# New orders of an audio tower's five engines, with PE's fillers ahead of the gate logits and the spread weights in four transfers

## What is computed

```python
patches = x[:, idx, :].reshape(B, 92, 512)
h = einsum('bpf,df->bpd', patches, W) + b
# attention, 8 heads of 64, on layernorm(h)
dots = einsum('bhid,bhjd->bhij', q, k) * scale
attn = softmax(dots)
attn = einsum('bhij,hg->bgij', attn, reattn_w)          # mixes the heads
attn = layernorm over the heads of attn * ln_g + ln_b
h = h + (attn @ v) @ w_out.T + b_out
# experts, on x = layernorm(h): two of eight for each token
scores = softmax(x @ gate_w.T);  topk_w, topk_i = top_k(scores, 2)
combine = topk_w / (sum(topk_w) + 1e-20), at topk_i
y = sum over e of combine[e] * (relu(x @ w1[e] + b1[e]) @ w2[e] + b2[e])
h = h + y + relu(x @ sw1 + sb1) @ sw2 + sb2
```

## Time and profile before

| what | value |
|---|---|
| median of 3 executions | 692.98 us (692.62 to 693.32) |
| the profiled execution, its own time | 693.01 us |
| its span | 691.2 us |
| PE busy | 646.2 us, 93% |
| DVE busy | 504.5 us, 73% |
| ACT busy | 446.1 us, 65% |
| POOL busy | 419.8 us, 61% |
| chain that ended last, by engine | PE 69%, DVE 21%, issue 3%, ACT 3%, POOL 2% |
| costliest group off PE | POOL act_split_lo, 127.5 us |
| spread, each | 1472 KB, 6.2 us from issue to landing |

### The profile page before, as it was taken

One profiled execution on the slowest core, in us unless ns is written; L12 is line 12 of the kernel. 1 busy time (PEld: TensorE's weight loads), 2 busy tenths in 40 slices (PEclk: granted clock), 3 DMA queues, 4 the chain that ended last, 5 costly groups with the idle time before them and its releaser, 6 DMA issues.

```text
span 691.2 us, 16491 instructions
## 1 busy us (share of the span) xinstructions
PE 646.2 (93%) x5918; PEld 591.8 (86%) x5918; DVE 504.5 (73%) x1432; ACT 446.1 (65%) x1430; POOL 419.8 (61%) x568
## 2 busy tenths in 40 slices
...
DMA packets 16753, 37.39 MB, mean 54 GB/s; under 512 B 1504, under 2 KB 13728, under 8 KB 14624
## 3 DMA queue, kind: packets, MB, share of 16 engines
...
...
## 4 chain that ended last, share of the span: by engine, by line
PE 69%; DVE 21%; issue 3%; ACT 3%; POOL 2%; DMA 1%; ACTq 0%; POOLq 0%; DVEq 0%
PE ps_mix L634 13%; PE ps_fill L414 12%; PE ps_fill L416 10%; PE ps_fill L415 10%; PE ps_dots L623 9%; PE ps_av L642 7%; PE ps_fill L563 5%; DVE key L1021 4%; DVE shift_l L1010 2%; DVE aT L1065 2%; DVE x2T_lo L1122 1%; PE ps_fill L734 1%; ACT x2T_hi L859 1%; DMA spread<-weights 1%; DVE hot L1016 1%
## 5 line engine op out<-in xcount | busy, mean ns | idle before, releaser
L486 POOL TENSOR_TENSOR act_split_lo<-act,act_split_hi 128x736 fp32r<-128x736 f32 (+1 forms) x80 | 127.5, 1603 | 15.0 <-ACT act_split_hi L842 15.0
L776 ACT ACTIVATE ex<-ps_dots,negmax 128x92 f32<-128x92 f32 x384 | 124.3, 342 | 6.9 <-DVE negmax L1046 6.5
L1194 POOL TENSOR_TENSOR sum<-sq 92x384 f32<-92x384 f32 x64 | 64.6, 1009 | 93.3 <-ACT sq L784 93.3
L634 PE MATMUL ps_mix<-mixk,probs 128*92 128x128 f32 x768 | 99.0, 280 | 11.4 <-DVE aT L1067 11.4
L1188 POOL TENSOR_TENSOR probs<-ex,rinv 128x552 f32<-128x552 f32 x64 | 71.0, 1109 | 51.9 <-DVE rinv L1052 51.9
L634 PEld LDWEIGHTS ps_mix<-mixk,probs 128*92 128x92 f32 x768 | 87.3, 162 | 17.3 <-issue 12.7
L1141 DVE SCALAR_TENSOR_TENSOR act<-ps_fill,b_neg,spread 128x368 f32<-128x368 f32 x128 | 70.5, 591 | 24.6 <-PE ps_fill L416 17.6
L776 ACT ACTIVATION_READ_ACCUMULATOR ex<-ps_dots,negmax 128x1 f32 x384 | 81.2, 212 | 0.0
L623 PE MATMUL ps_dots<-xT,yT 128*64 128x92 f32 x1536 | 74.5, 247 | 2.0 <-ACT ex L776 2.0
L623 PEld LDWEIGHTS ps_dots<-xT,yT 128*64 128x64 f32 x1536 | 64.9, 138 | 5.4 <-ACT ex L776 3.1
L1065 DVE TENSOR_TENSOR aT<-ps_mix,arstd 92x360 f32<-92x360 f32 x128 | 61.7, 522 | 6.8 <-ACT arstd L794 4.5
...
## 6 DMA issues: line engine op xcount, KB each, us to landing
spread<-weights SPq DMA_DIRECT2D x16, 1472.0 KB, 6.2
...
spread<-tok_raw SPq DMA_DIRECT2D x1, 256.0 KB, 3.5
```

The source lines that it names most:

```text
L486: eng.tensor_tensor(lo, act1[:, two, :], hi.bitcast(F32), ALU.subtract).then_inc(units_ready, 1)
L634: last = pe.matmul(ps_mix[0:N, c // HALF, o:o + 128], probs[:, (s - 1) % 2, c, :], mixk[:, :, :].rearrange("p g i -> p (g i)"), start=True ...
L776: last = act.activation(ex[:, s % 2, c, :], ps_dots[:, c // HALF, o:o + N], ACT.Exp, bias=negmax[:, c:c + 1], accum_out=sums[:, s % 2, c:c ...
L1194: pool.tensor_tensor(sum4[:, :, :, :], sq[:, :, 0:4, :], sq[:, :, 4:8, :], ALU.add)\
```

## The change

1. New orders in `SETUP`, `ORDER_0`, `STEPS` and `ORDERS_END`, and new counts in `KEEP_BUSY`.
2. The eight fillers stand ahead of `RT` instead of ahead of `CT`, in RT's bank (`FILL_BUSY`).
3. The logits are made by one reduce over the two rows of products instead of a copy and an add.
4. spread comes in four transfers of 368 KB, two experts each, each with a semaphore; the acts of an expert wait for its own.
5. In G = 17, the low halves of `H1` and `H3` are made on DVE instead of POOL (`VECTOR_UNITS`).

```diff
 STEPS = [
-    ("dots", 0), ("max", 0), ("av", 0), ("ev", 0), ("mix", 0), ("exa", 0), "Z5", "Z3", "Z2", ("sq", 0), ("exb", 0),
...
+    ("dots", 0), ("max", 0), ("exa", 0), "Z6", ("mix", 0), ("sq", 0), "Z5", "Z3", ("exb", 0), "Z2", "XE", ("inv", 0),
...
+VECTOR_UNITS = ("H1", "H3")
...
-ROUTE_BUSY = 8
...
+FILL_BUSY = {"RT": 8}
...
-                    sp.dma_start(spread[:, :, :].rearrange("p e w -> p (e w)"),
-                                 bass.AP(tensor=weights_dram.tensor, offset=0, ap=[[0, 128], [1, E * W]]))\
-                      .then_inc(weights_spread, 16)
+                    for k in range(E // 2):
+                        two = bass.AP(tensor=weights_dram.tensor, offset=2 * W * k, ap=[[0, 128], [W, 2], [1, W]])
+                        sp.dma_start(spread[:, 2 * k:2 * k + 2, :], two).then_inc(weights_spread[k], 16)
...
+                if FILL_BUSY.get(step, 0) and 0 <= g and G < LAST - 2:
+                    wait_free(pe, step, G)
+                    columns = w1_split[0][:, 0:4, :].rearrange("p e w -> p (e w)")
+                    for _ in range(FILL_BUSY[step]):
+                        pe.matmul(bank(step)[:, 0:W], columns[:, 0:128], columns[:, 0:W], start=True, stop=True)
+                if step == "CT":
+                    pe.wait_ge(route, N_ROUTE * (g + 1))
...
-                    columns = w1_split[0][:, 0:4, :].rearrange("p e w -> p (e w)")
-                    for _ in range(ROUTE_BUSY if g >= 0 and G < LAST - 2 else 0):
-                        pe.matmul(ps[:, 0:W], columns[:, 0:128], columns[:, 0:W], start=True, stop=True)
-                    pe.wait_ge(route, N_ROUTE * (g + 1))
...
-                    for ahead, unit in enumerate(units):
-                        pe.wait_ge(units_ready, len(UNITS) * g + ahead + 1)
+                    on_pool = [unit for unit in units if not on_vector(unit, G)]
+                    aside = [unit for unit in units if on_vector(unit, G)]
+                    for unit in units:
+                        if on_vector(unit, G):
+                            pe.wait_ge(vector_units, aside.index(unit) + 1)
+                        else:
+                            pe.wait_ge(units_ready, len(UNITS) * g + on_pool.index(unit) + 1)
...
-                    sums = bank("RT")[:, 0:2 * TILES * E].rearrange("p (t r e) -> p r t e", t=TILES, r=2)
-                    dve.tensor_copy(logit[:, :, :], sums[:, 1, :, :]).then_inc(logit_low, 1)
-                    dve.wait_ge(logit_low, g + 1)
-                    dve.tensor_tensor(logit[:, :, :], sums[:, 0, :, :], logit[:, :, :], ALU.add)\
-                       .then_inc(emptied[BANK["RT"]], 1)
+                    sums = bank("RT")[:, 0:2 * TILES * E].rearrange("p (t r e) -> p t e r", t=TILES, r=2)
+                    dve.tensor_reduce(logit[:, :, :], sums, AX_X, ALU.add).then_inc(emptied[BANK["RT"]], 1)
...
+                if on_vector(step, G):
+                    low_units(dve, step, G).then_inc(vector_units, 1)
...
-                    if step == [other for other in order(G) if other in EXPERTS][0]:
-                        dve.wait_ge(weights_spread, 16 * g + 16)
+                    experts = [other for other in order(G) if other in EXPERTS]
+                    if step == experts[0]:
                         at_least(dve, units_ready, len(UNITS) * g)
+                    if step == [other for other in experts if int(other[1]) // 2 == e // 2][0]:
+                        dve.wait_ge(weights_spread[e // 2], 16 * g + 16)
```

More of the change, by code:

```diff
@@ L32 @@
 N_ROUTE = 18
+ROUTED = {"RT": 2, "R2": 12, "R3": N_ROUTE}
 COPY = 32
@@ L75 @@
 STEPS = [
[8 rows of a table removed]
[3 rows of a table added]
+    "OP", ("rstd", 1), "shift", ("exa", 2), ("exb", 2), "TK", ("scale", 1), "TH2", "TH", "Z4", ("dots", 3),
[4 rows of a table added]
 ]
@@ L128 @@
 ORDER_0 = [
-    ("dots", 0), ("max", 0), ("exa", 0), ("exb", 0), ("inv", 0), "XE", "XO", "shift", "V3", ("dots", 1), ("max", 1),
-    ("mix", 1), ("exa", 1), ("sq", 1), ("exb", 1), "TK", ("rstd", 1), ("inv", 1), ("dots", 2), ("max", 2),
[3 rows of a table removed]
-    ("inv", 3), ("scale", 3), "BS",
+    "XE", "XO", "shift", ("dots", 0), ("max", 0), ("exa", 0), ("exb", 0), "TK", ("inv", 0), "V2", ("dots", 1),
+    ("mix", 1), ("max", 1), ("exa", 1), ("sq", 1), ("exb", 1), ("inv", 1), "TH", ("dots", 2), ("max", 2),
+    ("rstd", 1), ("exa", 2), ("exb", 2), ("scale", 1), "V3", "NH", ("mix", 2), ("sq", 2), ("dots", 3), ("max", 3),
@@ L144 @@
-    ("rstd", 3), ("av", 3), "hold", ("scale", 3), ("ev", 3),
-], [
-    "Z8", ("mix", 0), ("sq", 0), ("av", 0), ("ev", 0), "Z5", "H4", "Z1", "Z0", ("rstd", 0), ("scale", 0), "H0", "Z4",
-    "Z6", ("av", 1), ("ev", 1), "Z7", "OP", "H2", "Z2", "TH2", "Z3", "NH2", "H3", "TX2", "RT", "R2", "R3", "H1",
+    ("dots", 0), ("max", 0), ("mix", 0), "Z2", ("exa", 0), "Z3", "Z1", ("sq", 0), "Z7", ("exb", 0), "Z0", ("inv", 0),
+    ("dots", 1), ("max", 1), ("rstd", 0), ("av", 0), ("scale", 0), "Z6", ("ev", 0), "Z5", ("exa", 1), ("exb", 1),
```

34 lines of the change are left out of this document (21 added, 13 removed), and 22 rows, old and new, of tables (ORDERS_END, ORDER_0, STEPS).

## The result

The changed kernel takes 699.07 us (median of 7 executions, 695.86 to 702.46), the kernel before 693.0 (692.33 to 694.01): a ratio of 1.0087, 95% interval 1.0063 to 1.0112. It is slower, by 6.1 us. The profiled execution is the one of 699.07, its span 697.3. The forecast was 695.1 with a range of 686.5 to 700.5, and slower as the likeliest sign. But the time is not lost where the prediction had it, as the next lines show.

What follows compares the result with a forecast made beforehand. The prediction took the thirteen middle groups as deciding, bound by TensorE's work and VectorE's routing, which POOL's run holds. From 693.01, head -1.5, middle +6.5, G=15 and 16 +1.4 and G=17 -4.3 gave 695.1 us, range 686.5 to 700.5.

Steps and rivals of the forecast that it cites:

- signs of being right: Middle groups: hot over 1 us, shift_l over 1.2, combine ending some 14.6 after TH2 begins, PE waiting ahead of CT or mix3.
- Rival D: The forecast's middle, but the clock falls in G=1 and again in G=15, each 2.5 us: 699 us; chance 0.10.
- Middle, +6.5: Thirteen middle groups each lose 0.5 us through longer routing: +6.5 us in all (-6.5 to +12).
- step 5: Middle group's routing: the reciprocal, now behind shift_l, costs 0.2; key is held to 237.95 and hot to 239.5.
- step 4: POOL in a middle group: one unit joins the run ahead of sum, sum ends 0.85 later, shift_l is let go +0.8.
- PE's own work: TensorE in a middle group: its own work puts mix3 at 242.9 at the earliest, 0.7 from being the later chain.
- no group gains over 1.18: Middle groups: PE's work stays in its two windows, so TH2 to mix3 can't fall from 15.33 to under 14.15 us.
- Head, -1.5: G=-1, 0 and 1: new order loses 4.2 us at dots0, gives more back; -1.5 us (-3.2 to +1.5).
- The fall in G=1 that was given one half: TensorE's clock drops after 2.6 us idle ahead of CT in G=1, taking back 2 to 2.5 us; chance one half.
- G=15 and 16, +1.4: hot in G=15 is held some 1.7 us longer, shorter fillers of G=16 return 0.3: +1.4 us (0 to +3.5).
- G=17, -4.3: Last group: earlier first spread part -3.1, H1 and H3 on DVE about -1.3, less 0.1: -4.3 us (-3 to -5.5).
- the wrong theory: The prediction's view, tested in the experiments: middle groups cost 6.5 us, while the new head and end gain.

Runs made afterwards that it cites:

- inv_ahead: The changed kernel with the reciprocal (inv2) moved back ahead of RT in STEPS alone; 701.76 us, ratio to the kernel before 1.0107.
- h4_early: The changed kernel with the small POOL unit H4 moved in STEPS from the run ahead of sum to behind exb2, ahead of TK; 693.20 us.
- clock_fill: The changed kernel with twelve more fillers ahead of CT in G=1 and G=15, and 18 instead of 10 in G=17; 695.84 us.
- mid_only: The changed kernel with SETUP, ORDER_0, ORDERS_END and KEEP_BUSY of the kernel before and no low halves on VectorE; 700.08 us.
- old_head: The changed kernel with SETUP, ORDER_0 and the setup's fillers of the kernel before; 700.64 us.
- old_end: The changed kernel with ORDERS_END and the last groups' fillers of the kernel before, and no low halves on VectorE; 702.01 us.

## Why the prediction was right, and where it wasn't

The sign and the range held by luck: the terms were wrong one by one and offset each other. Nor did the prediction's own signs of being right show: hot took 0.42 and not over 1 us, shift_l 0.94 and not over 1.2, and combine ended 14.04 behind TH2 and not 14.6. Rival D comes nearest in number (699) and named two real causes, falls of the clock in G=1 and G=15, but it rests on the same wrong middle.

- **Middle, +6.5: wrong, -0.3 by the trace (twelve groups).** The step that failed is step 5, and with it the end of step 4: "shift_l is let go at 237.2". It was let in a whole sum earlier, at the joint of the third unit and sum. So hot met a pause, not sumsq and probs, and the last held op ended with probs, as before. POOL's run did end where forecast (11.81 behind TH2, forecast 11.75), and ten ops followed it, not thirteen. inv_ahead confirms it: in a middle group the reciprocal is worth 0, not 0.6.
- **PE's own work: right but for 0.3.** CT came at 14.48, 0.34 later, with 0.48 idle ahead of TH (forecast 0.64). The bound for mix3 was 15.15 behind TH2 (242.9); it stands at 15.29 in after, behind aT, and at 14.82 in h4_early, where it waits for nothing. The claim that no group gains over 1.18 stands: with PE's work kept, h4_early gained 0.57.
- **Head, -1.5: wrong, +3.8.** TH2 of G=1 was to come 2.0 earlier and came 2.4 later. Of these 4.4, 1.8 stand in dots0 already (a wait of 2.44 for M's bank, which the walk had shorter, and 1.2 GHz behind it), and part of the rest is the lower level behind 2.05 us of idle time in G=1. The fall in G=1 that was given one half did come, and cost 2.1 (clock_fill). Against the old head beside the same middle, though, the new one is 0.4 to 0.8 better by the traces.
- **G=15 and 16, +1.4: right in sign, +3.2.** hot was held for 4.54 where it was 2.82, the 1.7 of the forecast, and mix3 of G=15 came 0.9 later than before. Then the clock fell, of which there was nothing in the sum.
- **G=17, -4.3: mis-sized, -0.7.** The first part landed 3.7 behind its issue (3.4 taken), so the start was about right: 2.7 earlier, where 3.1 were forecast. What was missing is that later parts are waited for too, and that ten fillers in place of 25 let the clock fall, 1.2 us.
- **What no term held:** the 7.1 us that the new middle costs at its seams (mid_only). Of this, 1.5 us in the setup (2.4 up to TH2 of G=1) are shown to be the banks, and another 3.1 up to there go with the clock. What share of the rest is banks, order or clock stays open. No term of the prediction prices the new deal of banks in setup and end, and the clock is in its sum for G=1 alone.

That mid_only, old_head and old_end met the numbers of the wrong theory is the lesson of this case: total times alone would have confirmed it. The spacing of one row in each trace refuted it.
